# Score rows brought into a new partition order by GpSimd copies, with stores of 32 partitions and four batches

## The reference: what is computed

```python
r_feature            # (2048, 200, 64) float32
L0_rec_weight        # (200, 64, 64)   float32, 0.01 * normal

bilinear = jnp.einsum('bie,ied->bid', feature, weight)
out = jnp.einsum('bid,bjd->bij', bilinear, feature)     # (2048, 200, 200) float32
```

## Time and profile before

| | |
|---|---|
| three runs | 1517.48, 1518.4, 1518.64 us |
| profiled execution | 1516.77 us, of which the span is 1514.9 us |
| TensorE matmul busy | 1452.9 us (96% of the span) |
| VectorE busy | 1167.2 us (77%) |
| ScalarE busy | 893.5 us (59%) |
| GpSimd busy | 294.3 us (19%), nearly all of it issuing DMAs |
| DMA | 438.67 MB, mean 290 GB/s |
| granted TensorE clock | 0.998 of full speed |

### The profile page before, as it was taken

The page is one execution under the profiler, slowest core; times in us unless marked ns, Lnnn a source line. Parts: engine busy times, 40 slices in busy tenths (PEclk is TensorE's granted clock), DMA queues, the critical chain, the costliest instruction groups (busy, mean ns, idle before and its releaser), DMA issues.

```text
span 1514.9 us, 41346 instructions
## 1 busy us (share of the span) xinstructions
PE 1452.9 (96%) x16192; PEld 1206.3 (80%) x16192; DVE 1167.2 (77%) x2048; ACT 893.5 (59%) x1313; POOL 294.3 (19%) x518
## 2 busy tenths in 40 slices
PE   7999999999999999999999999999999999999965
PEld 6888887888788787888778888788787888878754
DVE  0578778788777778778787787877877777887897
ACT  5665665656656565665656656566665656656532
POOL 0112112121221212122121121221212111121222
PEclk9999999999999999999999999999999999999999
DMA  8799999999999999999999999999999999999898
GB/s 220 225 289 288 305 300 290 299 288 304 300 290 296 294 300 292 303 290 287 290 294 303 294 295 305 292 297 292 296 299 292 301 284 305 298 292 297 265 275 257
DMA packets 308574, 438.67 MB, mean 290 GB/s; under 512 B 56480, under 2 KB 255136, under 8 KB 308384
## 3 DMA queue, kind: packets, MB, share of 16 engines
q1 hardware_dynamic: 283808, 422.80, 87.1%
q0 software_dynamic: 24576, 13.24, 6.0%
HBM read 108.13 MB, written 327.68 MB: 288 GB/s over the span
## 4 chain that ended last, share of the span: by engine, by line
PE 83%; DVE 10%; DMA 3%; issue 3%; SPq 1%; ACT 0%; POOLq 0%
PE ps L225 43%; PE bp L209 24%; PE tp L193 14%; DVE staging L256 4%; DMA x<-feature_dram 3%; DVE win L305 3%; DVE win L312 2%; PE ps L209 1%; DVE win L313 1%; PE ps L193 1%; SPq L143 0%; SPq L138 0%; SPq L131 0%; ACT staging L256 0%; ACT bl L279 0%
## 5 line engine op out<-in xcount | busy, mean ns | idle before, releaser
L225 PE MATMUL ps<-win,bl 64*100 64x200 f32 x8192 | 831.7, 344 | 42.8 <-DVE win L313 39.6
L225 PEld LDWEIGHTS ps<-win,bl 64*100 64x100 f32 x8192 | 696.5, 207 | 134.3 <-issue 67.1
L256 DVE COPY staging<-ps 100x800 f32<-100x800 f32 x512 | 503.9, 984 | 252.2 <-PE ps L225 252.2
L256 ACT COPY staging<-ps 100x800 f32<-100x800 f32 x512 | 423.3, 827 | 251.9 <-PE ps L225 251.9
L176 POOL DMA_DIRECT2D out_dram<-staging x512 | 293.6, 573 | 1213.3 <-DVE staging L256 985.5
L209 PE MATMUL bp<-xt,w 64*64 64x128 f32 x6144 | 419.6, 276 | 0.0
L209 PEld LDWEIGHTS bp<-xt,w 64*64 64x64 f32 x6144 | 326.7, 133 | 65.2 <-issue 65.2
L279 ACT COPY bl<-bp 128x512 f32<-128x512 f32 x384 | 225.2, 586 | 178.0 <-PE bp L209 178.0
L269 ACT COPY xt<-tp 128x512 f32<-128x512 f32 x384 | 225.1, 586 | 171.4 <-PE tp L193 171.4
L305 DVE COPY win<-xt 128x400 f32<-128x400 f32 x512 | 272.9, 533 | 64.5 <-ACT xt L269 48.8
L193 PE MATMUL tp<-ident,x 128*128 128x128 f32 x1536 | 252.9, 287 | 7.9 <-DMA x<-feature_dram 7.6
(11 more groups left out here) (5 smaller groups left out, 0.6 us busy)
## 6 DMA issues: line engine op xcount, KB each, us to landing
out_dram<-staging SPq DMA_DIRECT2D x1024, 300.0 KB, 4.7
x<-feature_dram SPq DMA_DIRECT2D x400, 256.0 KB, 5.1
out_dram<-staging POOLq DMA_DIRECT2D x512, 25.0 KB, 4.6
w<-weight_dram SPq DMA_DIRECT2D x24, 128.0 KB, 3.9
w<-weight_dram SPq DMA_DIRECT2D x2, 64.0 KB, 3.3
```

Of the source, the lines that this page charges most:

```text
L225: last = nc.tensor.matmul(ps[s % TILES][0:FH, h, F * b:F * (b + 1)], rows_of_bl(n, R * k + PB * i + b)[64 * h:64 * h + 64], win[64 * h:64 ...
L256: copy(staging[:, slot, :, :, :].rearrange("p b h j -> p h b j"), ps[s % TILES][0:FH, :, 0:PB * F].rearrange("p h (b j) -> p h b j", j=F)) ...
```

## The change: what it does

A new tile `rows` has three slots, one for each quad in work. For every quad GpSimd copies the bilinear columns out of `bl` into a slot, which holds four batches of 128 places each. Pair 32 i + g (i = 0, 1, 2) goes to place 4 g + i, and pairs 96 to 99 go to places 3, 7, 11 and 15; the other 28 places stay zero. This takes two copies, one of 128 partitions by 384 elements (4 batches, 3 thirds, 32 pairs) and one of 16 elements. The stationary operand of `scores` is now a slot's batch: 128 columns side by side in every block. The output rows stand on 128 partitions in the order of the places, so a store of 32 pairs reads partitions i, i + 4, i + 8 and so on.

`staging` has seven slots of four batches. SyncE waits for both halves of a quad and then issues three stores of 32 partitions and four batches. GpSimd fills two quads of `rows` ahead and then, in turn, fills one more and stores the four last pairs of the quad just staged. TensorE waits for `rows_filled`; ScalarE's copy into `bl` for the next block waits for the quad's fill where it waited for its scores.

```diff
-    OSLOTS = 16
+    OSLOTS = 7
+    RSLOTS = 3
     WSLOTS = 3
     WG = 2
-    FA = FH // 16 * 16
+    THIRD = 32
+    PLACES = 4 * THIRD
+    FA = 3 * THIRD
...
-        staging = sbuf("staging", [FH, OSLOTS, PB, 2, F])
+        rows = sbuf("rows", [128, RSLOTS, R, PLACES])
+        staging = sbuf("staging", [PLACES, OSLOTS, R, 2, F])
...
-        def rows_of_bl(n, b):
-            return bl[:, 0:FH, b] if n % 2 == 0 else bl[:, b, 0:FH]
+        def quad_of_bl(n, k):
+            quad = slice(R * k, R * (k + 1))
+            return bl[:, 0:FH, quad].rearrange("p m r -> p r m") if n % 2 == 0 else bl[:, quad, 0:FH]
...
-            def store(s):
-                slot = s % OSLOTS
-                wait_staged(sp, s)
-                sp.dma_start(out_v[0:FA, PB * s:PB * (s + 1), :], staging[0:FA, slot]
-                             ).then_inc(out_written[slot], 16)
+            def store(q):
+                slot = q % OSLOTS
+                wait_staged(sp, 2 * q)
+                wait_staged(sp, 2 * q + 1)
+                for i in range(3):
+                    sp.dma_start(out_v[THIRD * i:THIRD * (i + 1), R * q:R * (q + 1), :],
+                                 staging[i:PLACES:4, slot].rearrange("p b h j -> p b (h j)")
+                                 ).then_inc(out_written[slot], 16)
...
-                    store(n * SETS_B + 2 * k)
-                    store(n * SETS_B + 2 * k + 1)
+                    store(n * QUADS + k)
...
+            def fill_rows(q):
+                n, k = q // QUADS, q % QUADS
+                if k == 0:
+                    pool.wait_ge(bl_stored, (n + 1) * NG)
+                if q >= RSLOTS:
+                    pool.wait_ge(scores_done, 2 * (q - RSLOTS) + 2)
+                places = rows[:, q % RSLOTS].rearrange("p r (g i) -> p r i g", i=4)
+                nc.gpsimd.tensor_copy(places[:, :, 0:3, :],
+                                      quad_of_bl(n, k)[:, :, 0:FA].rearrange("p r (i g) -> p r i g", i=3))
+                nc.gpsimd.tensor_copy(places[:, :, 3, 0:FH - FA], quad_of_bl(n, k)[:, :, FA:FH]
+                                      ).then_inc(rows_filled, 1)
+
+            nc.gpsimd.memset(rows[:], 0.0).then_inc(rows_cleared, 1)
+            pool.wait_ge(rows_cleared, 1)
+            for q in range(RSLOTS - 1):
+                fill_rows(q)
+            for q in range(BLOCKS * QUADS):
+                if q + RSLOTS - 1 < BLOCKS * QUADS:
+                    fill_rows(q + RSLOTS - 1)
+                store_rest(q)
...
-                if k == 0 and i == 0:
-                    pe.wait_ge(bl_stored, (n + 1) * NG)
                 if i == 0:
+                    pe.wait_ge(rows_filled, n * QUADS + k + 1)
                     pe.wait_ge(win_filled, n * QUADS + k + 1)
...
-                        last = nc.tensor.matmul(ps[s % TILES][0:FH, h, F * b:F * (b + 1)],
-                                                rows_of_bl(n, R * k + PB * i + b)[64 * h:64 * h + 64],
+                        last = nc.tensor.matmul(ps[s % TILES][0:PLACES, h, F * b:F * (b + 1)],
+                                                rows[64 * h:64 * h + 64, (n * QUADS + k) % RSLOTS, PB * i + b, :],
...
-                    act.wait_ge(scores_done, (n - 1) * SETS_B + 2 * t + 2)
+                    act.wait_ge(rows_filled, (n - 1) * QUADS + t + 1)
```

More of the change, by code:

```diff
@@ L36, in feature_interaction @@
     TILES = 3
-    OSLOTS = 16
+    OSLOTS = 7
+    RSLOTS = 3
     WSLOTS = 3
     WG = 2
-    FA = FH // 16 * 16
+    THIRD = 32
+    PLACES = 4 * THIRD
+    FA = 3 * THIRD
     assert 2 * E == 128 and B % NB == 0 and FH % C == 0 and NG <= QUADS and R == 2 * PB
-    assert PB * F <= 512 and C * NB == 512 and OSLOTS % 2 == 0 and (BLOCKS * SETS_B) % OSLOTS == 0
+    assert PB * F <= 512 and C * NB == 512 and FA < FH <= FA + THIRD
     feature_v = feature.rearrange("b f e -> b (f e)")
@@ L87, in feature_interaction @@
         bl_stored = sem("bl_stored")
+        rows_cleared = sem("rows_cleared")
+        rows_filled = sem("rows_filled")
         own_filled = sem("own_filled")
@@ L93, in feature_interaction @@
         out_written = [sem(f"out_written{i}") for i in range(OSLOTS)]
-        rest_written = [sem(f"rest_written{i}") for i in range(OSLOTS // 2)]
+        rest_written = [sem(f"rest_written{i}") for i in range(OSLOTS)]
         block = ctx.enter_context(nc.Block())
@@ L158, in _ @@
             for slot in range(OSLOTS):
[L159 to L162, removed]
+                uses = (BLOCKS * QUADS - slot + OSLOTS - 1) // OSLOTS
+                sp.wait_ge(out_written[slot], 48 * uses)
+                sp.wait_ge(rest_written[slot], 16 * uses)
         @block.gpsimd
@@ L170, in _, with store_rest @@
                                     ).then_inc(ident_ready, 1)
[L172 to L181, removed]
+            def store_rest(q):
+                slot = q % OSLOTS
+                wait_staged(pool, 2 * q)
+                wait_staged(pool, 2 * q + 1)
+                nc.gpsimd.dma_start(out_v[FA:FH, R * q:R * (q + 1), :],
+                                    staging[3:4 * (FH - FA):4, slot].rearrange("p b h j -> p b (h j)")
+                                    ).then_inc(rest_written[slot], 16)
+            def fill_rows(q):
[17 more added lines that the diff above has]
+                store_rest(q)
         @block.tensor
@@ L216, in scores @@
                 s = n * SETS_B + 2 * k + i
-                if k == 0 and i == 0:
-                    pe.wait_ge(bl_stored, (n + 1) * NG)
+                if n == 0 and k == 0 and i == 0:
+                    pe.wait_ge(rows_cleared, 1)
                 if i == 0:
+                    pe.wait_ge(rows_filled, n * QUADS + k + 1)
                     pe.wait_ge(win_filled, n * QUADS + k + 1)
@@ L249, in stage @@
         def stage(engine, copy, staged, s):
-            slot = s % OSLOTS
+            slot = s // 2 % OSLOTS
             engine.wait_ge(scores_done, s + 1)
-            used = s // OSLOTS
+            used = s // 2 // OSLOTS
             if used:
[L254 to L257, removed]
+                engine.wait_ge(out_written[slot], 48 * used)
+                engine.wait_ge(rest_written[slot], 16 * used)
+            copy(staging[:, slot, PB * (s % 2):PB * (s % 2 + 1), :, :].rearrange("p b h j -> p h b j"),
+                 ps[s % TILES][0:PLACES, :, 0:PB * F].rearrange("p h (b j) -> p h b j", j=F)
                  ).then_inc(staged, 1)
```

## The result

The changed kernel takes 1694.9 us (median of 4 runs, 1692.5 to 1696.5) against 1517.9 us for the kernel before: a ratio of 1.117, 95% interval 1.115 to 1.119. It is slower by 177 us where 8.5 us less were forecast.

What follows compares the result with a forecast made beforehand. TensorE was taken to bound most of the kernel, VectorE the last block and the block ends. The terms -11.7 + 3 + 1.2 - 1 = -8.5 us brought 1518.4 to 1509.9 us, range 1504 to 1515 us (48%).

Steps and rivals of the forecast that it cites:

- Loads of 128 adjacent columns: TensorE's loads for the scores: even blocks gain 2.03 us each, odd ones lose 0.65; net -11.7 us (-16.2 to +17).
- The size of GpSimd's copies: GpSimd's two copies per fill: together 0.8 us for an odd quad, 1.05 for an even one (0.5 to 1.5).
- Contention with VectorE: At block ends, fills of even quads outlast VectorE's 0.92 us of reading PSUM alone: +3 us (0 to +45).
- the one I priced (1536 us): Rival, 25%: fills of 1.3 us do not fit beside VectorE in 77 quads, costing 29 us; 1536 us.
- GpSimd becomes the bound: Rival, 6%: with copies of 2.0 us GpSimd's round of fill and store sets the pace, about 1697 us.
- The overhang: A fill's end running past VectorE's 0.92 us of reading PSUM alone: 0.13 us in 23 quads at block ends.
- Start: Before TensorE's first scores one fill now stands after ScalarE's last `bl`: +1.2 us once (0.5 to 1.8).
- Stores: SyncE's three stores a quad for two cost nothing; spread reads drain the queue sooner at the end: -1 us (-3 to +1).

Runs made afterwards that it cites:

- the run with the wait: The changed kernel, but GpSimd starts a fill only when VectorE has finished the round's win copies: 1499.5 us, ratio 0.989 to the kernel before.

## Why the prediction was wrong

*Loads of 128 adjacent columns*: right. 186 ns forecast, 187 measured; the longest usual matmul 434 forecast, 433 measured; blocks of 91.2 us forecast, 91.0 to 91.1 in the run with the wait, even and odd alike. In the run with the wait the first 15 blocks together are 14.6 us shorter than before, where -11.7 was forecast. The bound of -16.2 was too tight: if the 28 columns cost nothing, the even blocks gain 8 x 2.68 = 21.4 us. In the kernel after, this gain is hidden under VectorE's round.

*The size of GpSimd's copies*: inside the bounds for the large one, 0.90 us (0.41 to 1.21), and for the small one, 0.20 us unhindered. The 0.25 us more that I took for the pitched source of even blocks is not there: 0.90 us in even blocks, 0.89 in odd ones.

*Contention with VectorE*: this is the step that failed. I took from L313's 0.43 against 0.37 us that the two hinder each other a little, let the fill begin where the win copies end (414.75 in the earlier trace rows), and asked only whether its end fits. But the fill stands in GpSimd's queue right behind the store, and nothing keeps it back until 414.75: with the store over at 414.58 it falls into L313, which runs from 414.32 to 414.75. The overlap was in my own numbers, 0.17 us, and I gave it no price. The same holds for the quads with all of TensorE's work, of which the prediction says that VectorE idles or copies out of PSUM from 1.2 us on. The trace of the kernel before shows otherwise:

```profile
338.51 0.57 POOL L176 DMA_DIRECT2D out_dram<-staging  x1 [2.06 <-DVE staging L256]
...
338.80 0.45 DVE L313 COPY win<-win 64x400 f32<-64x400 f32 x1
...
339.98 0.99 DVE L256 COPY staging<-ps 100x800 f32<-100x800 f32 x1 [0.73 <-PE ps L225]
```

The store is over at 339.08, inside L313 (to 339.25), and so it is in 468 of the 512 quads of that trace. A fill right behind it had to fall on L313 nearly every time.

The price of the overlap is the whole of GpSimd's copy: L313's successor went from 0.43 to 1.38 us. I forecast +3 us with bounds of 0 and 45; measured between the kernel with and without the wait it is 195 us. The bound was wrong for the same reason: it counted only the 77 quads in which VectorE was last, but a round of 3.25 us makes VectorE last in nearly all 512.

By the Trainium skill (SBUF — State Buffer, section on who interferes with whom), as the prediction cites it, a copy on two ports and a GpSimd instruction exclude each other for the whole instruction. For a copy of 384 elements the trace of after agrees: 464 win copies, each over 0.22 to 0.24 us after GpSimd's. I had used the rule for the end of the fill and not for its start. For shorter copies the measurements differ from the rule, and they decide: beside 192 elements the win copy took 0.60 us and ended before GpSimd's did (in 466 of 479 rounds), and beside 96 it was not held.

*The rivals.* The one that came true is the contention, by another clash than the one I priced (1536 us): not at the end of the fill, but at its beginning. "GpSimd becomes the bound" has the time, 1697 us, but not the cause: GpSimd is busy 53% of the span, and the wait, which makes its round no shorter, took the 195 us away. The overhang itself was not there: 0.90 + 0.23 us left the last block of the run with the wait at 71.9 us.

*Start*: 53.04 against 51.55 us for the first scores, +1.5 where +1.2 was forecast; in the run with the wait 52.18, +0.6. *Stores*: SyncE's issue is 0.60 us at least where it was 0.32, which I had not foreseen, and still no stage waited for it. The drain is shorter than forecast. In the run with the wait the end comes 4.9 us after the last staging copy (1492.8 to 1497.7), before it was 8.2: -3.3 us, where -1 was taken with bounds of -3 and +1. That stores of 32 partitions are bearable in this kernel only with the spread places, the prediction did not see: it expected nothing of them but the drain.

With the clash removed the spans of the profiled executions differ by -17.2 us: -14.6 in the first 15 blocks, -0.5 in the last, -2.8 after it and +0.6 before the first scores. The forecast without its contention term was -11.7 - 1 + 1.2 = -11.5. Between the medians it is -14.9 us (1514.4 to 1499.5).

## What to carry to other kernels

Before giving GpSimd a copy, mark in VectorE's timeline the stretches in which it copies from SBUF to SBUF, and place the start as well as the end of GpSimd's copy against them: an overlap of 0.2 us can cost the length of the whole copy, every round. A wait on VectorE's last such copy, or copies of a quarter of the size, made the difference between 12% slower and 1% faster. Where TensorE waits for several signals, the releaser in the page may be a bystander; adding the suspect's work alone to the old kernel settles it in one run.

## What the runs showed of the hardware

- A VectorE copy of 64x400 elements from SBUF to SBUF and a GpSimd copy or memset hold each other up: 0.43 us became 1.38 us beside a copy of 384 elements and 1.28 beside a memset of 384, though the win copy had begun 0.26 us earlier. It became 0.60 us beside 192 and stayed at 0.43 beside 96. VectorE's copy out of PSUM was not lengthened (0.97 us).
- A GpSimd copy of 384 elements took 0.90 us, a memset of 384 elements four apart 0.81 us; in one dense memset of 1536 elements it was 1.37 us. ScalarE's copy of the same 384 took 0.90 us, where 512 elements out of PSUM take 0.59.
- Written side by side, GpSimd's copy of 400 elements took 0.52 us from adjacent elements and 0.88 us from elements 512 bytes apart.
- A store that reads every fourth partition took at least 0.60 us to issue on the SyncE queue, one from adjacent partitions 0.32 us, with medians of 0.60 to 0.61 us for both; but three stores of 32 adjacent partitions made the kernel 169 us slower than three spread ones.
